# A decoder layer on one core: the single last keys of all eight heads of a round in one score tile

## The reference, cut to what matters

```python
N, L, S, H, D = 8, 512, 1601, 16, 16
q = (queries @ Wq + bq).reshape(N, L, H, D)
k = (keys @ Wk + bk).reshape(N, S, H, D)
v = (values @ Wv + bv).reshape(N, S, H, D)
sm = jnp.einsum('nlhd,nshd->nlhs', q, k) / math.sqrt(D)
sm = jax.nn.softmax(sm, axis=1)
attn = jnp.einsum('nlhs,nshd->nlhd', sm, v).reshape(N, L, H * D)
```

## Time and profile before

| what | value |
|---|---|
| median of 3 runs | 2155.67 us |
| the profiled execution, its own time | 2156.47 us |
| its span, first to last instruction | 2154.6 us |
| mean granted TensorE clock | 0.961 |
| busy share of the span: PE, DVE, ACT, POOL | 92%, 80%, 70%, 35% |

### The profile page before, as it was taken

One profiled execution on the slowest core, in us unless ns is written; L12 is line 12 of the kernel. 1 busy time (PEld: TensorE's weight loads), 2 busy tenths in 40 slices (PEclk: granted clock), 3 DMA queues, 4 the chain that ended last, 5 costly groups with the idle time before them and its releaser, 6 DMA issues.

```text
span 2154.6 us, 43465 instructions
## 1 busy us (share of the span) xinstructions
PE 1978.6 (92%) x11070; PEld 1057.2 (49%) x11070; DVE 1717.4 (80%) x3255; ACT 1510.8 (70%) x4264; POOL 758.7 (35%) x1068
## 2 busy tenths in 40 slices
PE   7998998899999999999999998899739999999994
PEld 3554455323322233323322232333439999999994
DVE  6889886699999999999999999999535555555554
ACT  4665565799999999999999999999402323333233
POOL 0112111144444444444444442142453333333332
PEclk9989999899999999999999999999859999999997
DMA  4112103957677676867668585854632222222224
GB/s 159 44 44 73 59 25 108 218 107 109 122 120 125 129 101 134 133 112 127 104 134 132 113 142 123 153 93 95 176 111 33 39 35 36 36 37 37 37 37 168
DMA packets 135623, 211.13 MB, mean 98 GB/s; under 512 B 41026, under 2 KB 104258, under 8 KB 134354
## 3 DMA queue, kind: packets, MB, share of 16 engines
q1 hardware_dynamic: 107744, 150.18, 38.1%
q0 software_dynamic: 26240, 59.00, 10.4%
q10 hardware_dynamic: 1554, 1.05, 0.2%
HBM read 136.81 MB, written 73.74 MB: 98 GB/s over the span
## 4 chain that ended last, share of the span: by engine, by line
PE 42%; ACT 24%; issue 15%; DVE 11%; DMA 4%; SPq 2%; POOL 1%; ACTq 1%; DVEq 0%; POOLq 0%
ACT w_all L1843 20%; PE psum L2093 12%; PE psum L2103 11%; DVE neg_max L1681 7%; PE psum L658 6%; PE psum L1521 3%; PE psum L1465 3%; POOL list_all L341 1%; PE psum L1487 1%; DMA area<-x_all 1%; DMA vst<-v_all 1%; PE psum L2080 1%; SPq L387 1%; DMA v_all<-w_all 1%; ACT w_all L1007 1%
## 5 line engine op out<-in xcount | busy, mean ns | idle before, releaser
L1843 ACT ACTIVATE w_all<-psum,neg_max 128x512 f32<-128x512 f32 x1632 | 1094.8, 797 | 27.2 <-DVE neg_max L1681 24.8
L1681 DVE TENSOR_REDUCE neg_max<-psum 128x1 f32<-128x512 f32 x1600 | 980.4, 675 | 16.0 <-PE psum L1521 11.8
L1843 ACT ACTIVATION_READ_ACCUMULATOR w_all<-psum,neg_max 128x1 f32 x1632 | 517.4, 317 | 0.0
L1521 PE MATMUL psum<-qst,kst 96*128 96x512 bf16 x1536 | 467.9, 386 | 47.5 <-ACT w_all L1843 37.0
L2142 ACT ACTIVATE hid<-psum,b 128x128 f32<-128x128 f32 x568 | 162.5, 369 | 382.7 <-PE psum L2093 352.5
L1465 PE MATMUL psum<-w_all 128*32 128x512 f32 x3072 | 411.0, 608 | 1.5 <-DVE w_all L1697 1.5
L1521 PEld LDWEIGHTS psum<-qst,kst 96*128 96x128 bf16 x1536 | 120.8, 97 | 542.4 <-ACT w_all L1843 488.8
L1750 POOL TENSOR_TENSOR w_all<-vst,inv 128x64 f32<-128x64 f32 x384 | 108.7, 291 | 589.9 <-DVE inv L1607 589.4
L2093 PE MATMUL psum<-xst,w 128*128 128x128 f32 x2272 | 267.7, 276 | 0.0
L2093 PEld LDWEIGHTS psum<-xst,w 128*128 128x128 f32 x2272 | 261.9, 193 | 0.1
L2103 PE MATMUL psum<-area,hid 128*128 128x256 f32 x1136 | 256.9, 379 | 0.0
(11 more groups left out here) (231 smaller groups left out, 2095.5 us busy)
## 6 DMA issues: line engine op xcount, KB each, us to landing
kst<-k_parts SPq DMA_DIRECT2D x384, 112.0 KB
k_parts<-spare POOLq DMA_DIRECT2D x52, 336.0 KB, 2.9
w_all<-in_W SPq DMA_DIRECT2D x16, 1024.0 KB
area<-in_ctxT SPq DMA_DIRECT2D x16, 896.0 KB, 4.7
qst<-q_parts SPq DMA_DIRECT2D x192, 64.0 KB
v_all<-area POOLq DMA_DIRECT2D x13, 896.0 KB, 4.7
vst<-v_all SPq DMA_DIRECT2D x32, 224.0 KB
q_parts<-spare POOLq DMA_DIRECT2D x24, 256.0 KB, 3.0
```

Of the source, the lines that this page charges most:

```text
L1521: pe.matmul(psum[:, 2 * sbuf + i, :], kst[:, h, j, t * P:(t + 1) * P], qst[:, h, j, :], start=True, stop=True).then_inc(scores_ready, 1)
L1681: v.tensor_reduce(neg_max[:, sbuf, i:i + 1], psum[:, 2 * sbuf + i], AX_X, ALU.min) \
L1843: act.activation(probs_at[pb][:, j, :], psum[:, 2 * sbuf + i, :], ACT.Exp, bias=neg_max[:, sbuf, i:i + 1], scale=-1.0, accum_out=sums[:, t ...
```

## The change

One score bank a round holds the odd keys of all **eight** heads, made at tile 12; tile 25 makes none. For this, `odd_keys` holds, for each group g, a block of 32 weight columns for each head, all zero but column g, which is that head's odd key. PE makes the bank as two accumulating matmuls for each of the four strips. POOL copies the key columns in (`place_odd`): group 0's behind `scale_values(0)`, group 1's behind `scale_values(7)`, after a wait for the full load of that group. PE waits for both (`odd_placed`, which is the finished semaphore `wo_scaled` used again). The exponential goes to a buffer of its own (`odd_probs`), read by `pv` of tiles 12 and 25. The projected keys (`k1_out`) move out of `spare` to make room.

```diff
-                at = ODD_AT[j]
+                at = ODD_AT[j] + h
...
-            k1_out = spare[:, 0:2 * PARTS * KC].rearrange("p (i n s) -> p i n s", i=2, n=PARTS)
+            k1_out = w1_all[:, E - 1].rearrange("p c h -> p (c h)")[:, 0:PARTS * KC].bitcast(BF16) \
+                .rearrange("p (i n s) -> p i n s", i=2, n=PARTS)
+            odd_probs = spare[:, 2 * C * L:].bitcast(F32)
+            odd_keys = sb("odd_keys", [STACK, 2, GH, PAD], BF16)
+            odd_placed, ODD_BASE = wo_scaled, 1
...
-            score_buf = [k % SCORE_BUFS for k in range(N_SUB - 1)] + [1]
+            score_buf = [k % SCORE_BUFS for k in range(N_SUB - 1)] + [None]
+            ODD_TILE = ST - 1
+
+            def heads_of(tile, sub, i):
+
+                if tile == N_TILE - 1:
+                    return 3 if i == 1 else 1
+                return 2 if tile == ODD_TILE and sub == 1 else 1
...
                     if t == ST - 1:
+                        pe.wait_ge(odd_placed, 2 * (it + tile // N_TILE) + 2 + ODD_BASE)
                         pe.wait_ge(exp_done, head_free(k, 0, it))
                         for j in range(GH):
-                            last = pe.matmul(psum[ODD_AT[j]:ODD_AT[j] + PAD, 2 * sbuf, :],
-                                             kst[:, h, j, t * P + TAIL:t * P + TAIL + PAD], qst[:, h, j, :],
-                                             start=True, stop=True)
+                            for g in range(2):
+                                last = pe.matmul(psum[ODD_AT[j]:ODD_AT[j] + PAD, 2 * sbuf, :], odd_keys[:, g, j, :],
+                                                 qst[:, g, j, :], start=g == 0, stop=g == 1)
...
+                v.wait_ge(k_lo, KJ * FIRST_UNITS)
+                v.wait_ge(q_split, PARTS * B)
                 v.memset(sums[:], 1.0)
+                v.memset(odd_keys[:], 0.0)
...
+                def place_odd(tile, it):
+
+                    if tile in PLACE_AT:
+                        g = PLACE_AT.index(tile)
+                        at = (ST - 1) * P + TAIL
+                        wait_alone(pool, (heads_loaded[g], LOADS * (it + 1)))
+                        pool.tensor_copy(odd_keys[:, g, :, g:g + 1], kst[:, g, :, at:at + 1]).then_inc(odd_placed, 1)
+
+                PLACE_AT = (0, 7)
...
                     for tile in range(N_TILE):
                         scale_values(tile, it)
+                        place_odd(tile, it)
```

More of the change, by code:

```diff
@@ L1472, in pv @@
                             last = pe.matmul(psum[j * PAD:(j + 1) * PAD, 6, :], v_scaled[:, V_ODD, j, :],
-                                             probs_at[pb][:, 2, :], start=False, stop=True)
+                                             odd_probs, start=False, stop=True)
                     last.then_inc(pv_done, 1)
@@ L1506, in scores @@
                                                  start=True, stop=True)
-                            last.then_inc(scores_ready, 1)
+                            last.then_inc(scores_ready, heads_of(tile % N_TILE, sub, i))
+                        return
+                    if tile % N_TILE == N_TILE - 1:
                         return
                     if t == ST - 1:
+                        pe.wait_ge(odd_placed, 2 * (it + tile // N_TILE) + 2 + ODD_BASE)
                         pe.wait_ge(exp_done, head_free(k, 0, it))
                         for j in range(GH):
-                            last = pe.matmul(psum[ODD_AT[j]:ODD_AT[j] + PAD, 2 * sbuf, :],
-                                             kst[:, h, j, t * P + TAIL:t * P + TAIL + PAD], qst[:, h, j, :],
-                                             start=True, stop=True)
+                            for g in range(2):
+                                last = pe.matmul(psum[ODD_AT[j]:ODD_AT[j] + PAD, 2 * sbuf, :], odd_keys[:, g, j, :],
+                                                 qst[:, g, j, :], start=g == 0, stop=g == 1)
                         last.then_inc(scores_ready, 2)
@@ L1672, in tile_step @@
                             sbuf = score_buf[k % N_SUB]
-                            if tile % ST == ST - 1 and sub == 1:
+                            here = tile % N_TILE
+                            if here == N_TILE - 1 and sub == 1:
+                                continue
+                            if here == ODD_TILE and sub == 1:
                                 v.wait_ge(scores_ready, 2 * (N_SUB * it + k) + 2)
@@ L1681, in tile_step @@
                                 v.tensor_reduce(neg_max[:, sbuf, i:i + 1], psum[:, 2 * sbuf + i], AX_X, ALU.min) \
-                                    .then_inc(max_ready, 1)
+                                    .then_inc(max_ready, heads_of(here, sub, i))
                     if tile >= 2 and tile % 2 == 0 and not is_over(tile - 2, it):
@@ L1741, in attend_gpsimd @@
                 pool.wait_ge(q_stored, 16 * PARTS * B)
+                pool.wait_ge(x1_stored, 16 * B)
                 def scale_values(tile, it):
@@ L1762, in scale_values @@
                         v_scaled[:, V_ODD, :, 0:DH], vst[:, h, ST].rearrange("p (j d) -> p j d", j=GH),
-                        inv[:, tile, 2:3].rearrange("p (j o) -> p j o", o=1).to_broadcast([P, GH, DH]),
+                        inv[:, ODD_TILE, 2:3].rearrange("p (j o) -> p j o", o=1).to_broadcast([P, GH, DH]),
                         ALU.mult).then_inc(v_scaled_ready, 1)
+                def place_odd(tile, it):
[5 more added lines that the diff above has]
+                PLACE_AT = (0, 7)
                 def scale_rows(b, ts):
+                    if b == 0 and ts[0] == 0:
+                        for i in range(2):
+                            pool.wait_ge(k1_stored[i], 32 * FILLED)
                     if ts[0] == 0:
@@ L1802, in attend_gpsimd @@
                     scale_values(tile, FILLED + it)
+                    place_odd(tile, FILLED + it)
                     route_step(g)
@@ L1838, in tile_step @@
                         sbuf = score_buf[k]
-                        odd = tile % ST == ST - 1 and sub == 1
-                        for i in range(1 if odd else 2):
-                            j, heads = 2 * sub + i, 2 if odd else 1
+                        odd = tile == ODD_TILE and sub == 1
+                        for i in range(0 if sbuf is None else 1 if odd else 2):
+                            j, heads = 2 * sub + i, heads_of(tile, sub, i)
                             act.wait_ge(max_ready, 2 * (N_SUB * it + k) + i + heads)
-                            act.activation(probs_at[pb][:, j, :], psum[:, 2 * sbuf + i, :], ACT.Exp,
-                                           bias=neg_max[:, sbuf, i:i + 1], scale=-1.0,
+                            act.activation(odd_probs if odd else probs_at[pb][:, j, :], psum[:, 2 * sbuf + i, :],
+                                           ACT.Exp, bias=neg_max[:, sbuf, i:i + 1], scale=-1.0,
                                            accum_out=sums[:, tile, j:j + 1]).then_inc(exp_done, heads)
```

## The result

The changed kernel takes **2216.52 us** (median of 4 runs, 2214.51 to 2219.97) against 2154.93 of the kernel before (4 runs): a ratio of 1.0289, 95% interval 1.0274 to 1.0305. It is slower, as forecast, but 29.6 us slower than the 2186.9 forecast and 13.5 above the top of the range. The profiled execution took 2219.97 us.

The account below looks back on a forecast made before the run. ACT was taken to set the pace, with PE following. The terms, -10.6 - 4.7 + 44.2 + 2.3 = +31.2 on the profiled 2156.5, gave 2187.7, or 2186.9 us as median (that execution is 0.8 above it); range 2165 to 2203.

Parts of the forecast that it names:

- What bounds the kernel: Rounds 1 to 12: ACT sets the pace at 0.66 us a step, PE follows without slack, DVE is close behind.
- The exponential: ACT, all 16 rounds: one exponential in 102 goes, each round 0.66 us shorter, 10.6 us in all.
- The buffer out of turn: Start of rounds 1 to 12: the ring runs in turn, saving ACT 0.39 us each, 4.7 in all.
- POOL waits for a load: Tile 7, rounds 1 to 12: POOL stands 7.4 us for group 1's load, delaying PE and DVE; 44.2 us lost.
- the sum: All terms together, +31.2 us; its stall term for rounds 1 to 12 is 2 x 4.1 + 10 x 3.6 = 44.2.
- The odd matmuls: PE, tile 12: eight matmuls take between 0.45 and 1.1 us, hidden before tile 8's values come in rounds 1 to 12.
- Round 0: POOL at group 1's place: the load has landed before POOL arrives, so no wait and 0 us.
- Rounds 14 and 15: PE comes to tile 12 later while the load starts as early: 0 us, at the other end 2.3 each.
- Round 13: Copy, odd matmuls and pv stand behind a later load landing, so tile 13 comes 2.3 us later.
- The clock: Rival, chance 0.05: PE's new idle times around the odd matmuls lower its clock, 20 us more over twelve rounds, 2207.
- the stall's upper end of 56: POOL's wait in rounds 1 to 12 costs 56 us if its gap before the store is 1.7 each time, not 0.74.
- its edits there: Before the first scores: zeroing odd_keys and DVE's two waits cost 0, at most 0.3 us.

Follow-up runs that it names:

- the version kept busy: Changed kernel plus 5 and 10 matmuls that nothing reads, ahead of and behind the odd matmuls in rounds 0 to 12, POOL's wait kept: 2197.46 us.
- the version with no stall: Also called "both": changed kernel with group 1's odd keys placed at tile 9 and POOL waiting for queries and keys alone: 2148.89 us, ratio 0.9964.
- placed behind the piece: Changed kernel with POOL's wait and copy still in tile 7, but behind that tile's subtraction and store: 2167.60 us, ratio 1.0059.
- placed at tile 9: Changed kernel with group 1's odd keys placed behind the values of tile 9 instead of tile 7: 2170.12 us, ratio 1.0063.
- keys counted apart at tile 7: Changed kernel with POOL's wait still at tile 7, ahead of the piece, but for group 1's queries and keys alone: 2178.99 us, ratio 1.0101.
- both kernels without the change: The kernel before, 2154.93 us, and that kernel with only POOL's bare wait for group 1's full load added behind tile 7's values, 2228.05 us.

## Why the prediction was wrong, point by point

**What bounds the kernel**: right. One exponential added costs its step and a little more, one wait on PE goes whole into the round.

**The exponential, -0.66 a round**: right, measured 0.73 in rounds 1 to 12.

**The buffer out of turn, -0.39 a round**: too large. It measured 0.17 net, so 2.0 us over twelve rounds in place of 4.7. Whether the rest never was a loss, or is given back by the copy and the additional matmuls, no run tells apart. Both savings together came to 10.9 us over rounds 1 to 12 (825.7 to 814.9, before rounding); the terms said 12.6.

**POOL waits for a load**: right in each link. GpSimd's idle time was forecast as 7.4 and measured 7.71. `pv` of tile 8 was forecast 35.45 us behind the round's first exponential and came 35.56 behind it (1025.39 - 989.83). The idle times of PE were forecast as 1.9 and 1.7, and were 2.32 and 2.20 in round 8; over the twelve rounds the first was 1.3 to 2.3, the second 2.2, once 3.0. Taken by itself the stall is the version kept busy (861.7) less the version with no stall (814.9): 46.8 us, an upper bound since the filling may add to it, where the sum had 44.2.

**The odd matmuls**: hidden, as said. Eight of them let `pv` follow 0.43 us after their start (976.97 to 977.40, where nothing waits), the lower of the two bounds, 0.45.

**Round 0**: right, no wait. **Rounds 14 and 15**: together 2.4 shorter, of which 1.3 are the two exponentials.

**Round 13**: the size is near, 2.0 longer where 2.3 less the saving was forecast, but by luck. Busy time by stretch of round 13, before, after, and placed behind the piece, whose instructions are those of the changed kernel in this round:

```profile
1294.60:1370.00 75.40, 66.52 (x393) 21.38 (x394) 70.50 (x147) 71.16 (x213) 15.40 (x42) 1.00 0.74 145
1359.50:1436.90 77.40, 69.56 (x392) 21.88 (x384) 69.86 (x146) 70.65 (x211) 16.20 (x45) 0.96 0.71 141
1307.90:1382.30 74.40, 66.80 (x396) 21.39 (x392) 69.82 (x146) 70.20 (x211) 16.09 (x45) 1.00 0.71 147
```

With the clock at 1.00 the same round is 1.0 us shorter than before the change, not longer, though PE stands 1.62 us for the odd keys in it. In the changed kernel PE stood only 0.64 us for them, and two dips of 3.4 us stand in the round. The forecast delay of tile 13 by 2.3 us did not come: its scores began 36.9 us into the round there, and 35.0 with the copy placed behind the piece, against 35.9 before.

**The step that failed is the one that is missing from the sum: PE's new idle times cost nothing there but their own length.** The prediction had the mechanism, with both idle times, and gave it 0.05 as the rival *The clock*, because no row of rounds 1 to 12 had a dip and the rows with dips stood at the start of attention and in round 14. In fact every one of the twelve rounds had one: five times 3.4 us at half clock, seven times 6.8. Over rounds 1 to 12 the +60.7 are -10.9 saved, +46.8 stall at most and +24.8 clock at least. These add up by construction, since each is the difference of two kernels, so the size of the clock's part is checked by the rows: in round 8 the clock fell at 1024.1, 1.3 us before PE had work, so 5.5 us of work ran at half rate and lost 2.8. Reckoned so round by round, the seven long dips lose 2.2 to 3.1 each, 18.9 together; the five short ones began between 0.3 us before `pv` of tile 8 and 1.0 behind its start, and lose some 1.6 each. That is an estimate of 27 us, 2 above the lower bound, and leaves 44 for the stall, which is the 44.2 of the sum. The rival's own 2207 was still 9.5 short, by half because it took one short dip a round.

By the rule of the Trainium skill (TensorE: Matmul & The Clock Gate, What's actually happening), that idleness gates the array to half its rate, the time had to come out on the side of that rival; the trace agrees, with 0.50 in place of 1.00 from within the second of two idle times of 2.32 and 2.20 us.

**Weights.** A gap of 2 us twice in a round was a new thing for this stage, and where no row shows whether the clock survives one, the honest chance was nearer to a half than to 0.05. The range should have reached at least to 2207, and with the stall's upper end of 56 beyond it.

## What to carry to other kernels

A wait that an in-order engine makes for a transfer belongs behind all the work of that engine that others wait for, and on a count that covers only the bytes it needs: the same copy cost 49 us more ahead of one subtraction and its store than behind them, and at tile 9, with a count of the keys alone, it kept PE waiting no longer than before. Where a change opens idle time on PE in a stage whose granted clock was 1.00, price it twice, for its length and for a half clock behind it; filling the gap with matmuls that nothing reads tells the two apart, and gives a lower bound for the clock's part, since the filling can itself set the length, as it did here.

## What the runs showed of the hardware that was not expected

**The clock can fall behind short gaps in dense work.** Within rounds that are otherwise full, the granted clock went to 0.50 with two idle times, of 1.3 to 2.3 and of 2.2 us or more (all twelve rounds), with a single one of 3.8 to 4.9 (all twelve), and with a single one in only some rounds: 8 of twelve where it was 1.7 to 2.6 us, 4 where it was 1.2 to 1.9, 3 where it was 1.5 to 2.1. An idle time of 1.89 or 1.70 us was followed by it, one of 2.07 was not. What settles it in the border cases stays open. No dip came in rounds 1 to 12 where the longest idle times at tile 12 and 13 were 0.65 (kept busy, with one of 0.56 in one round) or 0.26 (both).

**A dip costs about half its length where PE has work throughout**: 1.7 to 1.9 us of a round for 3.4 us, in three kernels alike (rounds with a dip less rounds without, in the versions placed at tile 9, placed behind the piece, and keys counted apart at tile 7).

**The stage before moves.** The first exponential of attention stood between 399.9 and 405.0 us in the other nine profiles (before: 400.2). The shift is there ahead of the changed instructions: VectorE's sums of the mixer (L1141) that begin at 391.09 before begin at 395.75 after. But both kernels without the change are the two earliest, 399.9 and 400.2, and the eight with it begin at 400.7 to 405.0, so whether the change has a part in it (the prediction gave its edits there at most 0.3) is not shown. Spans of two profiles can differ by 5 us for the start of attention alone; distances between the rounds' first exponentials are the cleaner measure, equal to 0.1 us over undisturbed rounds.
